# A selective scan whose GpSimd product with C takes two tiles at a time, and whose C arrives in pairs

## What is computed

```
def step(h, inp):
    d, u, Bv, Cv = inp
    dA = jnp.exp(d[..., None] * A)
    h = h * dA + (d * u)[..., None] * Bv[:, :, None, :]
    return (h, jnp.einsum('bkdn,bkn->bkd', h, Cv))
```

## Time and profile before

| | us |
|---|---|
| median of 3 runs | 6276.51 |
| lowest and highest run | 6275.66, 6281.68 |
| profiled execution: span from first to last instruction | 6270.2 |
| GpSimd, products with C (L918), 1536 | 2749.4 busy, 1824 ns each |
| VectorE, scans (L883) with carry and both kinds of input | 1.79 each, 1.73 in a fresh chunk |
| VectorE, hard products (L862), 576 | 546.6 busy, 949 ns each |
| GpSimd, driven inputs (L912), 192 | 348.7 busy, 1816 ns each |
| first scan starts, last scan starts | 796.6, 4082.0 |

### The profile page before, as it was taken

One profiled execution on the slowest core, in us unless ns is written; L12 is line 12 of the kernel. 1 busy time (PEld: TensorE's weight loads), 2 busy tenths in 40 slices (PEclk: granted clock), 3 DMA queues, 4 the chain that ended last, 5 costly groups with the idle time before them and its releaser, 6 DMA issues. The chain is left out here.

```text
span 6270.2 us, 83748 instructions
## 1 busy us (share of the span) xinstructions
PE 5167.0 (82%) x21564; PEld 3423.2 (55%) x21564; DVE 4275.8 (68%) x4244; ACT 3892.7 (62%) x8375; POOL 4196.6 (67%) x2703
## 2 busy tenths in 40 slices
PE   4666389999898898998989999845589999965997
PEld 2333155555555555555555555522358888844776
DVE  2666589999999999999999999956231111143433
ACT  2655488888888888888888888834532222233233
POOL 0566589999999999998999999933014444412343
PEclk8888599999999999999999999977789999975898
DMA  3454477777777777777777777764200000013213
GB/s 94 148 186 181 183 241 250 248 248 247 243 250 239 249 247 244 248 247 238 247 246 247 251 246 249 243 216 164 91 18 0 0 0 0 0 38 107 70 58 128
DMA packets 399686, 1073.56 MB, mean 171 GB/s; under 512 B 51470, under 2 KB 94511, under 8 KB 393600
## 3 DMA queue, kind: packets, MB, share of 16 engines
q1 hardware_dynamic: 384544, 1038.35, 49.7%
q0 software_dynamic: 7584, 20.72, 1.0%
q10 hardware_dynamic: 7104, 9.44, 0.5%
HBM read 883.39 MB, written 184.94 MB: 170 GB/s over the span
## 5 line engine op out<-in xcount | busy, mean ns | idle before, releaser
L918 POOL TENSOR_TENSOR scan_hc<-scan_h,scan_c_rep 128x768 f32<-128x768 f32 x1536 | 2749.4, 1824 | 236.7 <-PE scan_ps_y L749 171.4
L749 PE MATMUL scan_ps_y<-scan_hc,keep_ident 128*128 128x512 f32 (+1 forms) x6144 | 2217.2, 489 | 23.5 <-ACT scan_y L784 23.1
L883 DVE TENSOR_TENSOR_SCAN scan_h<-scan_da,scan_h,scan_ps_p 128x768 f32<-128x768 f32 x896 | 1567.8, 1794 | 0.0
L749 PEld LDWEIGHTS scan_ps_y<-scan_hc,keep_ident 128*128 128x128 f32 x6144 | 1066.6, 190 | 822.5 <-issue 737.6
L801 ACT ACTIVATE scan_warm<-scan_du_t 128x128 f32<-128x128 f32 x4608 | 1423.7, 388 | 40.7 <-PE scan_ps_p L740 35.3
L840 ACT ACTIVATE scan_da<-scan_dd,layer_a_neg 128x768 f32<-128x768 f32 x1344 | 1184.2, 921 | 2.2 <-issue 1.6
L1260 POOL TENSOR_TENSOR attn_e_lo<-attn_e,attn_e_hi 128x512 fp32r<-128x512 f32 x324 | 417.6, 1289 | 771.4 <-DVE attn_e_hi L1251 771.4
L740 PE MATMUL scan_ps_p<-keep_ident,scan_warm 128*128 128x128 f32 x4608 | 645.9, 277 | 221.9 <-DVE scan_h L883 221.1
L883 DVE TENSOR_TENSOR_SCAN scan_h<-scan_da,scan_ps_p 128x768 f32<-128x768 f32 x448 | 758.4, 1734 | 2.1 <-ACT scan_da L840 2.0
L740 PEld LDWEIGHTS scan_ps_p<-keep_ident,scan_warm 128*128 128x128 f32 x4608 | 531.5, 142 | 371.8 <-issue 160.4
L862 DVE TENSOR_TENSOR scan_ps_p<-scan_ps_p,scan_dd 128x768 f32<-128x768 f32 x576 | 546.6, 949 | 185.9 <-PE scan_ps_p L732 185.0
(11 more groups left out here) (291 smaller groups left out, 7109.4 us busy)
## 6 DMA issues: line engine op xcount, KB each, us to landing
scan_c_rep<-bc_dram SPq DMA_DIRECT2D x1536, 384.0 KB, 4.1
scan_dd<-dd_dram SPq DMA_DIRECT2D x96, 768.0 KB, 5.6
scan_b_rep<-bc_dram SPq DMA_DIRECT2D x192, 384.0 KB, 4.7
dd_dram<-delta_de SPq DMA_DIRECT2D x96, 384.0 KB, 6.5
dd_dram<-delta_du SPq DMA_DIRECT2D x96, 384.0 KB, 15.7
y_dram<-scan_y SPq DMA_DIRECT2D x96, 384.0 KB, 4.5
merge_y<-y_dram SPq DMA_DIRECT2D x32, 1152.0 KB, 10.3
delta_img<-xn_dram SPq DMA_DIRECT2D x16, 576.0 KB, 10.1
```

The source lines that it names most:

```text
L749: mm = pe.matmul(ps_y[:, lo:hi], keep["ident"][:, :], hc[t % HR][:, lo:hi], start=n == 0, stop=n == N - 1)
L883: dve.tensor_tensor_scan(view(h[n]), view(x), view(y), start, ALU.mult, ALU.add).then_inc(scan_done, 1)
L918: pool.tensor_tensor(hc[t % HR][:, :], h[t % N][:, :], c_rep[t % CR][:, :], ALU.mult).then_inc(hc_done, 1)
```

## The change

GpSimd's product takes two tiles in one instruction of 1536 columns. For that the state buffers `h` and the products `hc` are laid out in pairs (eight `h2`, four `hc2` instead of six single ones), and C is loaded as a pair of rows, 768 KB, into one of three pair buffers (the same memory as the six single ones). The product is issued at the odd tile of a pair. It waits for the scan of the odd tile, the pair of C, and the sums of the pair that had the same buffer four pairs before; it counts 2 on `hc_done` at its end. SyncE's load for a pair stands at the even tile and waits until the product three pairs before is done. TensorE, VectorE and ScalarE have the same instructions and waits as before.

```diff
--- before.py
+++ after.py
@@ -597,19 +597,20 @@
     with ExitStack() as ctx:
         s = Space(nc, ctx, "scan")
         ring = lambda name, n, shape=(128, WC), dt=F32: [s.sb(f"{name}{i}", list(shape), dt) for i in range(n)]
-        CR, SR, PR, HR, DR, WR = 6, 2, 3, 6, 4, 2
+        CR, SR, PR, HR, DR, WR = 6, 2, 3, 8, 4, 2
         dd = ring("dd", 2, (128, 2, WC))
         cut = ring("cut", 2, dt=F32R)
-        c_rep, b_rep = ring("c_rep", CR), ring("b_rep", SR)
+        c_rep, b_rep = ring("c_rep", CR // 2, (128, 2, WC)), ring("b_rep", SR)
         da, bu = ring("da", DR), ring("bu", SR)
         rows = ring("rows", 2, (N, WC))
         du_t = ring("du_t", 2, (128, WC + NB * N))
         warm = ring("warm", WR, (128, NB, 128))
-        h, hc, y = ring("h", N), ring("hc", HR), ring("y", 2)
+        h2, hc2, y = ring("h", N // 2, (128, 2, WC)), ring("hc", HR // 2, (128, 2, WC)), ring("y", 2)
+        h, hc = [h2[n // 2][:, n % 2, :] for n in range(N)], [hc2[n // 2][:, n % 2, :] for n in range(HR)]
         ps_p = [s.ps(f"ps_p{i}", [128, 1024]) for i in range(PR)]
         ps_y = s.ps("ps_y", [128, 1024])
         dd_here = [s.sem(f"dd_here{i}") for i in range(2)]
-        c_here = [s.sem(f"c_here{i}") for i in range(CR)]
+        c_here = [s.sem(f"c_here{i}") for i in range(CR // 2)]
         b_here = [s.sem(f"b_here{i}") for i in range(SR)]
         y_out = [s.sem(f"y_out{i}") for i in range(2)]
         cut_clear, spread_done, ex_done, mult_done, bu_done, scan_done, hc_done, sum_done, y_taken = (
@@ -686,9 +687,11 @@
                             load_b(u, ahead, first)
                         elif not last:
                             load_b(u + 1, ahead - TILES, False)
-                    if not (first and t < CR):
-                        sp.wait_ge(hc_done, at - CR + 1)
-                    sp.dma_start(c_rep[t % CR][:, :], P["bc"][u, k, 1, n, cn * WC:cn * WC + WC].partition_broadcast(128)).then_inc(c_here[t % CR], 16)
+                    if t % 2 == 0:
+                        if not (first and t < CR):
+                            sp.wait_ge(hc_done, at - CR + 2)
+                        q = t % CR // 2
+                        sp.dma_start(c_rep[q][:, :, :], P["bc"][u, k, 1, n:n + 2, cn * WC:cn * WC + WC].partition_broadcast(128)).then_inc(c_here[q], 16)
 
             for q in range(2):
                 sp.sem_inc(y_out[q], 16)
@@ -912,10 +915,11 @@
                 pool.tensor_tensor(bu[f % SR][:, :], dd[st % 2][:, 1, :], b_rep[f % SR][:, :], ALU.mult).then_inc(bu_done, 1)
 
             def weigh(u, t):
-                pool.wait_ge(scan_done, u * TILES + t + 1 + 3)
-                pool.wait_ge(c_here[t % CR], u * (16 * TILES // CR) + 16 * (t // CR) + 16)
-                pool.wait_ge(sum_done, u * TILES + t + 1)
-                pool.tensor_tensor(hc[t % HR][:, :], h[t % N][:, :], c_rep[t % CR][:, :], ALU.mult).then_inc(hc_done, 1)
+                q = t % CR // 2
+                pool.wait_ge(scan_done, u * TILES + t + 2 + 3)
+                pool.wait_ge(c_here[q], u * (16 * TILES // CR) + 16 * (t // CR) + 16)
+                pool.wait_ge(sum_done, u * TILES + t + 2)
+                pool.tensor_tensor(hc2[t % HR // 2][:, :, :], h2[t % N // 2][:, :, :], c_rep[q][:, :, :], ALU.mult).then_inc(hc_done, 2)
 
             def unit(u, first, last):
                 for t in range(TILES):
@@ -929,7 +933,8 @@
                             drive(u, ahead, first)
                         elif not last:
                             drive(u + 1, ahead - TILES, False)
-                    weigh(u, t)
+                    if t % 2:
+                        weigh(u, t - 1)
 
             pool.sem_inc(sum_done, HR)
             unit(0, True, False)
```

## The result

The changed kernel takes 6736.55 us (median of 4 runs, 6732.83 to 6750.84) against 6278.77 of the kernel before: ratio 1.0729, 95% interval 1.0713 to 1.0745. It is slower, as forecast, by twice what was forecast: 458 us where 226 stood, and outside the range of 6385 to 6580. Its profiled span is 6731.8 us, 461.6 more than before.

A forecast was written before the change was run, and what follows sets the result against it. VectorE, TensorE and three PSUM slots bound the scan, with rows arriving without slack; 94 steps x 2.4 us of later rows = 226 us on the 6270.2 span, plus 6.3 to the median: 6502 us, +3.6%, range 6385 to 6580.

The forecast's parts named there:

- What bounds the kernel: Scan step of 34.2 us: the loop of VectorE, TensorE and three PSUM slots sets it; GpSimd follows.
- The pair's 0.2 us each: GpSimd's eight pair products a step: 1.6 us less busy, gaining 0 since nothing waits for its products.
- The pair's product: GpSimd's product of 1536 columns: 3.39 us, between 3.3 and 3.59; tiles 0 and 1 released 1.2 us later.
- The burst: SyncE's queue after pair 0-1: C, B, dd, cut and rows go out together, so the rows land later.
- Three quarters of the way: Landing of the next step's rows, taken at 3047.5, between 3046.43 and 3047.86.
- upper end: Latest landing of the rows, 3047.86: both additional 384 KB pass first, 2.03 us at 387 GB/s.
- From flip to product: TensorE's turn of next input to VectorE's product of tile 10: 1.93 us after a late flip, against 2.36; 0.43 absorbed.
- From the product to the end of the next scan 15: VectorE behind the product of tile 10: runs on through its scans, the remaining delay passed on whole, nothing added.
- GpSimd was not the bound: Rival: GpSimd bounds the scan after all, so the change is faster, at most 154 us, 6123; chance 0.05.
- the landing did move: Rival: the rows' landing doesn't move, or the flip's delay stays under 0.43 us, so no change, 6277; chance 0.08.
- the pair's product did not cost more than two singles: Rival: GpSimd's pair product takes 4.0 us, costing 3.6 us a step, 338 us, 6615; chance 0.04.
- The signs named beforehand: Expected in the new trace: flip waits about 2.5 us, VectorE idles 3 us at tile 10, GpSimd waits for scan_h.

The follow-up runs named there:

- experiments 1 and 10: Changed kernel with the next step's loads at tile 6 instead of 8: 6274.74 us, ratio 0.9993; the same with FLIP = 11 too: 6191.49 us, ratio 0.9856.
- Experiment 6: Changed kernel with its pair products, but C loaded one tile at a time into the halves of the pair buffers: 6627.29 us, ratio 1.0557.
- experiment 4: Changed kernel with 14 transposes of the identity on TensorE before the flip's wait for the loads: 6651.16 us, ratio 1.0595.

## Why the prediction was half right

*What bounds the kernel: right.* VectorE, TensorE and the three PSUM slots set the step; GpSimd follows. The pair's 0.2 us each were rightly costed at 0, and experiments 1 and 10 show it.

*The pair's product: right.* 3.39 us in a row was taken; three in a row take 10.34 and one 3.45, so 3.45. Pair 0-1 is released 1.2 to 1.3 us later than tile 1 was.

*The burst: right in kind, too small.* "Three quarters of the way, 3047.5", 19.0 us after scan 15, was 20.12. Its upper end, 3047.86 or 19.4 us, was not an upper end. It added the bytes at the rate of the busy stretch, 387 GB/s, to a landing of before. What it left out is that the rows fare worse behind C as one transfer of 768 KB than behind two: the rows' load is issued 0.65 us later than by adding issues up (11.67 against 11.0), and the landing takes 8.5 us, 0.5 more than the 8.0 forecast. Experiment 6, with the same bytes in single transfers, has 0.94 us from dd to rows and a landing of 7.8, near both figures; it lands at 19.50 and not at 19.0 because it has one more issue ahead.

*From flip to product: the step that failed worst.* "The product 1.93 after the flip" was read from a step in which TensorE had waited for 0.96 us. In the changed kernel it waits 4 us, and the time is 3.04 between the medians, as the granted clock behind the wait falls to 0.50. The forecast put the clock at nothing. It need not have: the trace of before has a flip that waited the 2.3 us which the earlier trace rows names as the longest, and it was slow in the same way, 2875.94-2872.90 = 3.04 us from flip to product. TensorE and VectorE in that step, and the stretch from flip to product (columns as in the earlier trace rows):

```profile
2872.90 1.32 PE L721 MATMUL scan_ps_p<-keep_ident,scan_dd 128*128 128x128 f32 x6 [2.35 <-DMA scan_rows<-bc_dram]
...
2875.94 0.97 DVE L862 TENSOR_TENSOR scan_ps_p<-scan_ps_p,scan_dd 128x768 f32<-128x768 f32 x1 [3.87 <-PE scan_ps_p L732]
```

```profile
2872.90:2876.00 3.10, 3.10 (x15) 2.63 (x16) 0.06 (x1) 0.99 (x2) 1.40 (x1) 0.54 0.98 367
```

*The parts together,* by means over the 94 steps, after less before. The flip starts 3.77 us later (16.53 to 20.30), where the forecast had 2.86. From flip to product it is 0.72 longer (2.16 to 2.88), where the forecast had 0.43 *shorter*. From the product to the end of the next scan 15 it is 0.44 longer (15.56 to 16.00), which the forecast put at nothing; experiment 4 leaves 0.26 of it, and no run takes the rest apart. So of the 2.5 us missing, 0.9 are the rows' landing, 1.15 the way from flip to product and 0.44 what follows: 2.4+0.9+1.15+0.44 = 4.9 us a step; 94 steps make 461, the difference of the spans.

*The rivals.* None came. GpSimd was not the bound, the landing did move, and the pair's product did not cost more than two singles.

*The signs named beforehand* came in kind: the wait at the flip in practically all steps (4 us, not 2.5), VectorE's idle at tile 10 (5.4 us, not 3), GpSimd waiting for scan_h, scans still at 1.79, and a landing of 8.5 us where 7.5 to 8.5 stood. The rows' issue, expected 10.9 to 11.2 after scan 15, came at 11.67, outside.

## What to carry to other kernels

A merged instruction on an engine that nobody waits for bought nothing here, busy share of 94 to 97% or not, and the release it gives in one piece can cost: look for what stands on an in-order queue behind that release, and whether it arrives with any slack now. Where a load lands within 0.1 us of the moment it is wanted, issue it earlier before anything else is touched; here moving it and its consumer by a tile or two is worth 1.6%, and the pair 0. And when a wait grows, the price of the work behind it must be read from a row behind a long wait, not from one behind a short one: the longest wait in the list of the kernel before was one such row.

## What was not expected of the hardware

Behind a wait of 4.3 us TensorE's granted clock was 0.50 in the step shown, and six turns of 128 columns took 1.45 us instead of 0.87, a spread 1.01 instead of 0.61; over 94 such steps the mean clock from flip to product was 0.60. 1.75 us of work without use in such a wait, with 3 us of idleness left behind it, was enough in the step shown to have the flip at 0.88, and lifted that mean to 0.89. One transfer of 768 KB for C ahead of a step's loads, with B's of 384 KB between, let the rows land 0.6 us later than two of 384 KB did, and the issue of the rows took 2.17 us in the step shown and 0.53 at the median, instead of 0.37 and 0.38.
